# Four gated convolution-style layers on one core: where the projections take their reciprocals

## The reference

```python
x = x + layer(_gn(x))                     # _gn: group norm over pairs of channels

xn = layernorm(x)                         # over the 64 channels of one position
left  = (xn @ W_left  + b_left)  * mask * sigmoid(xn @ W_lgate + b_lgate)
right = (xn @ W_right + b_right) * mask * sigmoid(xn @ W_rgate + b_rgate)
out_gate = sigmoid(xn @ W_ogate + b_ogate)
out = einsum('bkid,bkjd->bijd', left, right)      # 256 x 256 products for each channel
out = layernorm(out) * out_gate
return out @ W_out + b_out
```

## Time and profile before

| what | value |
|---|---|
| median of 3 executions | 1584.8 us (1577.82 to 1585.05) |
| profiled execution, its own time | 1581.19 us |
| its span, first to last instruction | 1579.4 us |
| mean granted TensorE clock | 0.955 of full speed |
| TensorE matmul busy | 1385.7 us, 88% |
| VectorE busy | 1216.6 us, 77% |
| ScalarE busy | 978.5 us, 62% |
| GpSimd busy | 447.7 us, 28% |
| reciprocals of the projections (L930) | 12, 40.2 us in total |

### The profile page before, as it was taken

One profiled execution on the slowest core, in us unless ns is written; L12 is line 12 of the kernel. 1 busy time (PEld: TensorE's weight loads), 2 busy tenths in 40 slices (PEclk: granted clock), 3 DMA queues, 4 the chain that ended last, 5 costly groups with the idle time before them and its releaser, 6 DMA issues. The chain is left out here.

```text
span 1579.4 us, 26738 instructions
## 1 busy us (share of the span) xinstructions
PE 1385.7 (88%) x9158; PEld 775.1 (49%) x9163; DVE 1216.6 (77%) x2069; ACT 978.5 (62%) x1578; POOL 447.7 (28%) x387
## 2 busy tenths in 40 slices
PE   6769897878897997899989999898889979997997
PEld 5417432222674442345569997222245547772443
DVE  6644787699799886789957777896789968997664
ACT  5675588634344888677846665356767856662555
POOL 6300397320001992310000000695320000002665
PEclk9898998999999998999999999998999989997999
DMA  9368210056884220589988886793169889995998
GB/s 360 119 197 294 94 54 1 1 161 205 290 309 162 94 68 1 172 308 335 343 317 306 301 307 229 267 380 150 60 265 345 342 331 384 418 391 194 383 407 321
DMA packets 152693, 381.62 MB, mean 242 GB/s; under 512 B 15728, under 2 KB 15984, under 8 KB 152432
## 3 DMA queue, kind: packets, MB, share of 16 engines
q1 hardware_dynamic: 140176, 356.64, 62.2%
q10 hardware_dynamic: 12384, 23.28, 4.0%
HBM read 191.11 MB, written 188.74 MB: 241 GB/s over the span
## 5 line engine op out<-in xcount | busy, mean ns | idle before, releaser
L1182 PE MATMUL banks<-work 128*128 128x256 f32 x1408 | 334.7, 386 | 16.2 <-DVE work L1255 6.3
L1182 PEld LDWEIGHTS banks<-work 128*128 128x128 f32 x1408 | 261.1, 195 | 62.9 <-issue 17.9
L734 PE MATMUL banks<-work,w 64*64 64x512 f32 x2048 | 262.7, 603 | 12.5 <-DVE work L961 9.6
L1542 POOL TENSOR_TENSOR xT<-xT,work 128x512 f32<-128x512 f32 x192 | 241.0, 1272 | 57.3 <-DVE work L1591 54.3
L961 DVE SCALAR_TENSOR_TENSOR work<-banks,bias,work 128x512 f32<-128x512 f32 x256 | 188.5, 748 | 38.2 <-PE banks L734 31.4
L850 ACT ACTIVATE work<-banks,bias 128x512 f32<-128x512 f32 x256 | 171.7, 685 | 56.4 <-PE banks L734 56.2
L1214 ACT COPY work<-banks 128x512 f32<-128x512 f32 x176 | 103.2, 586 | 140.6 <-PE banks L1182 139.1
L734 PEld LDWEIGHTS banks<-work,w 64*64 64x64 f32 x2048 | 104.9, 134 | 128.0 <-DVE work L961 80.6
L1353 POOL MEMSET work<- 32x2048 bf16 x4 | 7.2, 1799 | 562.1 <-issue 461.4
L1281 DVE TENSOR_TENSOR work<-work 128x512 f32<-128x512 f32 x176 | 121.2, 689 | 58.3 <-ACT work L1214 57.1
L1591 DVE SCALAR_TENSOR_TENSOR work<-banks,bias,work 128x512 f32<-128x512 f32 x192 | 142.0, 748 | 28.4 <-ACT work L1516 15.1
(11 more groups left out here) (170 smaller groups left out, 2201.2 us busy)
## 6 DMA issues: line engine op xcount, KB each, us to landing
hidden_rows<-work SPq DMA_DIRECT2D x128, 512.0 KB, 4.1
work<-hidden_rows SPq DMA_DIRECT2D x120, 512.0 KB, 6.0
products<-work SPq DMA_DIRECT2D x88, 512.0 KB, 3.8
work<-products SPq DMA_DIRECT2D x88, 512.0 KB, 4.8
work<-gate_rows SPq DMA_DIRECT2D x64, 512.0 KB, 5.6
work<-hidden SPq DMA_DIRECT2D x40, 512.0 KB, 6.0
work<-in_x SPq DMA_DIRECT2D x32, 512.0 KB, 5.2
gate_rows<-work SPq DMA_DIRECT2D x32, 512.0 KB, 3.1
```

The source lines that it names most:

```text
L734: mm = pe.matmul(out[side, :], w(name)[rows, side], h[rows, t % H, :], start=True, stop=True)
L1182: mm = pe.matmul(ZB[c % 2][:, r * N:r * N + N], a[:, kk, rows_of(r, c)], x[:, kk, :], start=(kk == 0), stop=(kk == 1))
L1542: pool.tensor_tensor(columns(t), columns(t), term[:, t % RING, :], ALU.add).then_inc(x_sb, 1)
```

## The change

In `project` alone:

- `inverse(1)` moves from ahead of `squares(26)` to behind all squares, ahead of `normed(0)`.
- In the stacked layers 2 and 3, `inverse(2)` is issued as eight reciprocals of 64 columns, one behind each of the pairs 2 to 9, and `inverse(3)` as eight behind the pairs 13 to 20. In layer 1 both stay whole: `inverse(2)` behind pair 2 as before, `inverse(3)` behind pair 6 and not 4.
- `sd` gets three slots, so `variance(x)` waits for `split` >= 4(x - 2). `high`, the buffer of the split's rounded part, goes from two slots to one.

```diff
-    H, RP, SLOTS = 4, 3, 8
+    H, RP, SLOTS, SD = 4, 3, 8, 3
+    PIECES = 8 if stacked else 1
...
-    sd, at = core.area([2, T], at)
+    sd, at = core.area([SD, T], at)
     rec, at = core.area([T], at)
-    high, at = core.area([2, T], at, BF16)
+    high, at = core.area([T], at, BF16)
...
+    def pieces_until(x):
+
+        return x + 1 if x < 2 else 2 + PIECES * (x - 1)
...
             for x in range(SETS_OF_ROOTS):
-                rest = sd[:, x % 2, :]
-                pool.wait_ge(rec_sb, x + 1)
-                pool.tensor_scalar(high[:, 0, :], rec, later[0], None, ALU.mult).then_inc(split, 1)
+                rest = sd[:, x % SD, :]
+                pool.wait_ge(rec_sb, pieces_until(x))
+                at_least(pool, split, 4 * x)
+                pool.tensor_scalar(high, rec, later[0], None, ALU.mult).then_inc(split, 1)
...
             def variance(x):
                 dve.wait_ge(mean_sb, x + 1)
-                at_least(dve, split, 4 * (x - 1))
-                var = sd[:, x % 2, :]
+                at_least(dve, split, 4 * (x - SD + 1))
+                var = sd[:, x % SD, :]
...
-            def inverse(x):
-                dve.wait_ge(sd_sb, x + 1)
-                at_least(dve, split, 4 * x)
-                dve.reciprocal(rec, sd[:, x % 2, :]).then_inc(rec_sb, 1)
+            def inverse(x, piece=0, pieces=1):
+                if piece == 0:
+                    dve.wait_ge(sd_sb, x + 1)
+                    at_least(dve, split, 4 * x)
+                part = slice(piece * T // pieces, (piece + 1) * T // pieces)
+                dve.reciprocal(rec[:, part], sd[:, x % SD, part]).then_inc(rec_sb, 1)
...
-                    if u == 2 * last_step(x) + 8:
+                    if x == 0 and u == 2 * last_step(x) + 8:
                         inverse(x)
                 squares(u)
+            inverse(1)
...
-                if u in (2, 4):
-                    inverse(SETS_OF_ROOTS - 3 + u // 2)
+                for x, first in ((2, 2), (3, 5 + PIECES)):
+                    if first <= u < first + PIECES:
+                        inverse(x, u - first, PIECES)
```

More of the change, by code:

```diff
@@ L845, in root @@
                 act.wait_ge(var_sb, 2 * x + 2)
-                nc.scalar.activation(sd[:, x % 2, :], sd[:, x % 2, :], ACT.Sqrt, bias=eps).then_inc(sd_sb, 1)
+                nc.scalar.activation(sd[:, x % SD, :], sd[:, x % SD, :], ACT.Sqrt, bias=eps).then_inc(sd_sb, 1)
             def sigmoid(n, name, t, column):
@@ L897, in _ @@
             for x in range(SETS_OF_ROOTS):
-                rest = sd[:, x % 2, :]
-                pool.wait_ge(rec_sb, x + 1)
-                pool.tensor_scalar(high[:, 0, :], rec, later[0], None, ALU.mult).then_inc(split, 1)
+                rest = sd[:, x % SD, :]
+                pool.wait_ge(rec_sb, pieces_until(x))
+                at_least(pool, split, 4 * x)
+                pool.tensor_scalar(high, rec, later[0], None, ALU.mult).then_inc(split, 1)
                 pool.wait_ge(split, 4 * x + 1)
-                pool.tensor_tensor(rest, rec, high[:, 0, :], ALU.subtract).then_inc(split, 1)
+                pool.tensor_tensor(rest, rec, high, ALU.subtract).then_inc(split, 1)
                 pool.wait_ge(split, 4 * x + 2)
-                pool.tensor_scalar(high[:, 1, :], rest, later[1], None, ALU.mult).then_inc(split, 1)
+                pool.tensor_scalar(high, rest, later[1], None, ALU.mult).then_inc(split, 1)
                 pool.wait_ge(split, 4 * x + 3)
-                pool.tensor_tensor(parts[:, x, :], rest, high[:, 1, :], ALU.subtract).then_inc(split, 1)
+                pool.tensor_tensor(parts[:, x, :], rest, high, ALU.subtract).then_inc(split, 1)
         @block.vector
```

## The result

The changed kernel takes 1556.1 us (median of 4 runs, 1549.9 to 1559.2), the kernel before beside it 1584.0. The ratio is 0.983, 95% interval 0.981 to 0.985: faster by 27.8 us. The forecast was 1561, range 1552 to 1573. A second set of runs gave 1554.3 us and 0.984 (0.982 to 0.985).

A forecast was written before the change was run, and what follows sets the result against it. TensorE was taken to pace the pairs of layers 2 and 3, VectorE briefly the front. Gains 7.4 + 1.2 + 5.5 + 7.2 = 21.3 us gave 1559.9 (profiled) or 1563.5 (median), stated as 1561; own range 1555 to 1567, wider 1552 to 1573.

The forecast's parts named there:

- Front, what the move releases: Fronts of the three projections: squares follow `variance(1)` at once, TensorE's 3.44 us stand goes; 14.8 us together if nothing else is late.
- Front, what is late next: Fronts: GpSimd's split ends 2.38 us later, delaying `inverse(1)`, and variances run late; gains 2.7, 2.6, 2.0, together 7.4 us.
- the rival without hold-up: Fronts: GpSimd and VectorE interleave, so the front gives 14.8 us and the kernel takes 1554; chance 0.15.
- Third slot: Front of layer 3: the third `sd` slot removes the 1.12 us that `variance(3)` waited for the split.
- Layer 1: Pairs of layer 1: the fourth reciprocal, behind pair 6, no longer waits 1.23 us for set 2; 1.2 us gained (0.5 to 2).
- What goes: Pairs of layers 2 and 3: the stalls around the whole reciprocals, 7.1 us in layer 2 and 8.8 in layer 3.
- What the pieces cost: Pairs of layers 2 and 3: each piece holds VectorE 0.52 us, 0.1 exposed; 1.6 us per layer (bounds 0 and 8.3).
- TensorE's clock: Fronts: TensorE stands for the variances instead, so its clock level may vary; 1.5 us per layer either way.
- my four terms: Front 7.4, pairs of layer 1 1.2, net pairs of layer 2 5.5 and of layer 3 7.2: 21.3 us.
- Exposed pieces: Rival, pairs of layers 2 and 3: each piece adds its 0.52 us; the sum is 7.9 us, time 1575; chance 0.12.
- DMA in layer 2: Rival: at 0.98 busy the stores can't follow and pairs wait for buffers; 5.5 us less gain, 1567; chance 0.07.
- a large fixed cost of the reciprocal: Rival "slower": pieces exposed at the upper price of 1.07 us each lose 34 us, giving 1592; chance 0.04.

The follow-up runs named there:

- one_port: Changed kernel, but VectorE's squares of pairs 26 and 30 take their second factor from PSUM instead of SBUF (output differs): 1556.9 us in one run.
- two_slots: Changed kernel with two slots for the variances (`sd`) instead of three: 1565.6 us, ratio 0.988.
- pieces_only: Kernel before plus only the eight-piece reciprocals in layers 2 and 3 and the one slot of `high`: 1567.4 us, ratio 0.989.
- pieces_4: Changed kernel with four pieces of 128 columns per reciprocal in layers 2 and 3 instead of eight of 64: 1558.6 us, ratio 0.984.

## Why the prediction was right, and where it was not

**Front, what the move releases: right.** TensorE's 3.4 us at step 13 are gone, and `factors(0)` comes as computed.

**Front, what is late next: the wrong step.** I moved the end of GpSimd's split of set 0 by the squares' 2.38 us, said that it makes no difference which of the two gets in first, and so had `inverse(1)` start 6.1 us behind L925 of the second variance. It started 4.63 us behind in layer 1 (294.62 to 299.25), 4.62 in layer 2 and 3.83 in layer 3, where it had been 3.73. GpSimd's operation was in first and was not held up; it held up the squares by 1.45 us in layers 1 and 2, and there was room for that: TensorE wanted `squares(26)` 3.8 us after they began, and VectorE would have waited 0.75 us for the factors without it (one_port). Which of the two engines waits decides what it costs. The contention itself was forecast and one_port shows it. Of the two L925 behind the first `h` tiles, the first met L902's successor at 1.21 to 1.23 us in layers 1 and 2, as said (1.18), and the second ran free (0.43); in layer 3 the first ran free and the second took 0.85. I had both late, 1.1 us in all.

Counted from `inverse(0)` to the second h tiles (layer 1) or the first factors of the pairs (2 and 3), the fronts gained 4.7, 5.0 and 4.3 us: 14.0, where I had 7.4 and the rival without hold-up 14.8. Counted to the second `h` tiles in all three, which is where the forecast ended, it is 4.7, 4.6 and 4.3, 13.6.

**Third slot: right.** Its 1.12 us in layer 3 became 2.9 to 4.1 us per layer once the move had brought the variances forward (two_slots).

**Layer 1: the wait went, the gain is not shown.** The fourth reciprocal no longer waits. I counted its 1.2 us as gained because VectorE ran without a gap from there on. That was misread: it has gaps before and after the change, as ScalarE waits for stores, 8.2 us in four places before. From the second h tile to the end the projection gained 0.9 us, but in the six profiles with the changed kernel's layer 1 this stretch takes 93.3 to 97.3 us, and 94.2 and 95.9 in the two with the old one (before and pieces_only). 1.5 us were lost ahead of `inverse(0)`, where the trace shows only a longer wait for TensorE's first steps; the second execution of the same kernel again differs, so I put it to scatter.

**What goes: right.** Layers 2 and 3 lost 7.1 and 8.8 us; they are back to within 0.05 us of the steady pace.

**What the pieces cost: the term was too large.** I had 0.52 us of hold and 0.1 exposed, 1.6 us per layer. Measured: 0.46 and 0.05 us per layer. The 0.5 us absorbed, read from the kernel before, was the right threshold: pieces_4 gives 0.49.

**TensorE's clock: it stayed up.** In the changed kernel TensorE stands 1.47 us for the fourth variance of layer 2 and 1.28 in layer 3, and the granted clock stays at 1.00; before, behind the 3.44 us of standing, it was 0.59 from 302 to 306 us in layer 1 and 0.50 from 634 to 637 in layer 2, and 1.00 in layer 3.

The projections gained 28.6 us where my four terms gave 21.3, so 1561 stands 5 us too high: 6.6 us too little for the fronts and 3.1 for the pairs of layers 2 and 3 (15.8 and not 12.7), less what layer 1 did not show and scatter. The time fell into the range although the front was forecast at half of what it gave. The trace's own span, 22.3 us shorter, would have looked like a perfect hit and is not one: 6.3 us of scatter elsewhere lies on it.

Of the rivals, the front without hold-up came nearest, and with 1554 nearer to the measured 1556.1 than my 1561. Its reason does not hold: the engines did hold each other up, 3.83 us instead of 2.38, but where it cost next to nothing. The time alone would have spoken for the wrong mechanism. Exposed pieces, DMA in layer 2, and a large fixed cost of the reciprocal all fell.

## What to carry to other kernels

Before cutting a long operation up, read how late the engine behind it becomes when it is held once: the part of the hold that does not come out is the largest piece that hides, and one step above it (0.86 against 0.46 us) the cost returns in every turn. When work is moved beside an engine that holds it up, as GpSimd does VectorE here, ask which of the two will be in first, and whether the one that then waits has room. And bring the buffers along: a move that runs ahead of its ring is taken back there.

## What the runs showed that I had not expected

- Eight reciprocals of 64 columns in a row take 3.34 us, one of 512 columns 3.27. In a row the fixed part nearly vanishes; I had taken 0.13 us from elementwise rows. The Trainium skill, VectorE: DVE Perf Modes, section "The TRN2 errata — SBUF-src ops pay a fixed extra latency per instruction", gives 0.06 us and more for each further instruction and advises against small tiles; for this reciprocal the runs differ in a row, 0.01 us; between other operations they give 0.06 start to start, which agrees, and the 0.09 us by which the operation behind each piece is shorter takes it back.
- GpSimd won against VectorE in between two back-to-back squares in some places and not in others: in layers 1 and 2 L906 waited for both squares (3.55 us), in layer 3 of the changed kernel for one (2.44, the two squares then 2.81 instead of 2.38). The ten profiles in which `inverse(1)` has moved have thirty fronts. Four of them went that second way, and the same code in another execution did not. So in the fronts neither price is fixed.
- Cutting paid off in layer 1 as well, where VectorE has only 0.1 us of a 2.49 us pair to spare.
